# Layer one of a graph network: eight rows of every group are fetched by SyncE in place of GpSimd

## What is computed

```python
def _rgcn_layer(x, W, SW, b, src, dst, rel):
    xt = jnp.einsum('nd,rde->rne', x, W)          # 8 relations
    msg = xt[rel, src]                            # one row of 128 for each edge
    agg = jax.ops.segment_sum(msg, dst, num_segments=x.shape[0])
    return jax.nn.relu(agg + x @ SW + b)
x = _rgcn_layer(entity_emb, w1, sl1, b1, src, dst, edge_type)
x = _rgcn_layer(x, w2, sl2, b2, src, dst, edge_type)
```

## Time and profile before

| | us |
|---|---|
| median of 3 executions | 8923.19 |
| lowest, highest | 8923.06, 8924.19 |
| profiled execution, total | 8924.33 |
| profiled execution, span from first to last instruction | 8922.3 |
| of it layer one's gathers, first start to last start | 120.9 to 2196.9 |

### The profile page before, as it was taken

How to read it: one execution, slowest core, us unless ns; L and a number is a source line. 1 busy time by engine, 2 the same in 40 slices (tenths; PEclk the granted TensorE clock), 3 DMA queues, 4 the chain that set the end, 5 groups by cost and what they waited for, 6 DMA issues and landing times. The chain is left out here.

```text
span 8922.3 us, 172430 instructions
## 1 busy us (share of the span) xinstructions
PE 6527.5 (73%) x29604; PEld 5175.7 (58%) x29605; DVE 5892.7 (66%) x18026; ACT 2572.9 (29%) x6876; POOL 6456.8 (72%) x6759
## 2 busy tenths in 40 slices
PE   6555555555788888888888988888745677666667
PEld 4433333333555555555688888888734566666555
DVE  4444444444566666666688888888854776766767
ACT  3111111111011111111355555555433333333322
POOL 6777777776777777777677777777757777777752
PEclk7566666666555555555555555555556777877778
DMA  5222222222222222222455555555435666666652
GB/s 199 61 65 67 66 65 66 66 65 64 54 63 62 62 63 62 62 63 62 102 137 136 136 136 136 136 136 136 121 81 126 154 154 152 156 154 154 154 139 77
DMA packets 1031683, 926.16 MB, mean 104 GB/s; under 512 B 210913, under 2 KB 911477, under 8 KB 1031495
## 3 DMA queue, kind: packets, MB, share of 16 engines
q0 software_dynamic: 214496, 443.25, 18.3%
q1 hardware_dynamic: 627671, 341.67, 15.1%
q10 hardware_dynamic: 189400, 139.98, 7.8%
HBM read 734.34 MB, written 192.49 MB: 104 GB/s over the span
## 5 line engine op out<-in xcount | busy, mean ns | idle before, releaser
L599 PE MATMUL stage_ps_agg<-stage_hot,stage_msg 128*128 128x128 f32 x6656 | 1587.4, 414 | 1221.6 <-DMA stage_msg<-xt,stage_index 890.7
L599 PEld LDWEIGHTS stage_ps_agg<-stage_hot,stage_msg 128*128 128x128 f32 x6656 | 1377.5, 306 | 1519.2 <-issue 662.4
L1174 POOL DMA_INDIRECT big<-q,stage_index x1664 | 1597.2, 960 | 547.3 <-issue 489.0
L1631 POOL DMA_INDIRECT slots<-big,stage_index x1664 | 1603.2, 963 | 510.6 <-issue 442.0
L588 POOL DMA_INDIRECT stage_msg<-xt_next,stage_index x1664 | 1570.7, 944 | 531.0 <-issue 520.3
L588 POOL DMA_INDIRECT stage_msg<-xt,stage_index x1664 | 1570.3, 944 | 530.3 <-issue 487.6
L631 DVE TENSOR_TENSOR big<-big,stage_ps_agg 128x128 f32 x3328 | 951.7, 286 | 1350.5 <-PE stage_ps_agg L599 989.8
L577 ACT ACTIVATE stage_index<-big 128x4 int32 (+1 forms) x832 | 170.3, 205 | 3607.3 <-PE stage_ps_agg L599 3509.1
L1668 PE MATMUL stage_ps_val<-nodes_a,big 128*128 x3328 | 672.4, 366 | 656.8 <-ACT big L1594 635.1
L1668 PEld LDWEIGHTS stage_ps_val<-nodes_a,big 128*128 128x128 f32 x3328 | 592.4, 267 | 719.0 <-issue 718.3
L1684 PE MATMUL stage_ps_sums<-stage_hot,big 128*128 128x128 f32 x4160 | 754.9, 345 | 112.0 <-DVE big L1804 107.1
(11 more groups left out here) (306 smaller groups left out, 9675.2 us busy)
## 6 DMA issues: line engine op xcount, KB each, us to landing
big<-slots SPq DMA_DIRECT2D x1976, 66.0 KB
big<-in_edge_attr_dram SPq DMA_DIRECT2D x1664, 64.0 KB
stage_trow<-targets ACTq DMA_DIRECT2D x830, 128.0 KB
stage_msg<-xt,stage_index POOLq DMA_INDIRECT x1664
stage_msg<-xt_next,stage_index POOLq DMA_INDIRECT x1664
big<-q,stage_index POOLq DMA_INDIRECT x1664
slots<-big,stage_index POOLq DMA_INDIRECT x1664
xt_next<-stage_xo SPq DMA_DIRECT2D x98, 256.0 KB, 2.9
```

The costliest lines, as they stand in the source:

```text
L599: last = self.nc.tensor.matmul(self.ps[h][:, j, :], self.msg[q][:, j, :], self.hot[h][:, j, :], start=True, stop=True)
L1174: pool.indirect_dma_start(qrow[q][:, j * D:(j + 1) * D], None, d["q"], bass.IndirectOffsetOnAxis(ap=index[q][:, j:j + 1], axis=0))\
L1631: pool.indirect_dma_start(d["slots"], bass.IndirectOffsetOnAxis(ap=index[q][:, j:j + 1], axis=0), total[q][:, j, :], None).then_inc(s_sc[q ...
```

## The change

`prepare` makes a second small table: VectorE copies the last eight (`SIDE`) lanes' row numbers of every tile from `row` into `side` as integers, and SyncE writes that to HBM as its last transfer. `first_layer` begins with a SyncE transfer that brings the eight numbers of each group's fourth tile into one partition of on-chip memory (`side_rows`).

In layer one's `gather` the fourth indirect DMA of a group covers partitions 0 to 119. SyncE fetches the other eight rows (`load_side_rows`): it waits until the slot is free, twice loads four row numbers into registers, and issues eight DMAs of one row each on a semaphore of the slot. TensorE waits for that semaphore besides the gathers'. SyncE's program for the layer is now written by `walk_edges` as well, and the store of a job stands in it two groups after ScalarE's copy. Layer two is as before.

```diff
+SIDE = 8
 # prepare, SyncE
+        sp.wait_ge(s_v, SIDED)
+        sp.dma_start(d["side"].rearrange("(c p) l -> p c l", p=P), side[:, :, :]).then_inc(s_tab, 16)
...
-        sp.wait_ge(s_tab, 32)
+        sp.wait_ge(s_tab, 48)
 # prepare, VectorE
         v.wait_ge(s_v, NUMBERED)
+        nc.vector.tensor_copy(side[:, :, :], row[:, :, P - SIDE:P]).then_inc(s_v, 1)
 # Layer.gather
                 for j in range(G):
-                    pool.indirect_dma_start(self.msg[q][:, j, :], None, self.xt,
-                                            bass.IndirectOffsetOnAxis(ap=self.index[q][:, j:j + 1], axis=0))\
+                    rows = P - self.side if j == G - 1 else P
+                    pool.indirect_dma_start(self.msg[q][0:rows, j, :], None, self.xt,
+                                            bass.IndirectOffsetOnAxis(ap=self.index[q][0:rows, j:j + 1], axis=0))\
                         .then_inc(self.s_msg[q], 16)
+    def load_side_rows(self, sp, x):
+
+        q = x.slot()
+        sp.wait_ge(self.s_freed, x.at() + 1)
+        for k in range(0, SIDE, G):
+            r = offsets(self.nc, mybir.EngineType.SP, self.t["side_rows"], x.at() * SIDE + k, G, W * P * R - 1)
+            for j in range(G):
+                p = P - SIDE + k + j
+                sp.dma_start(self.msg[q][p:p + 1, G - 1, :], self.xt[bass.ds(r[j], 1), :]).then_inc(self.s_side[q], 16)
 # Layer.sum_messages
         pe.wait_ge(self.s_msg[q], x.turn() * (16 * G) + (16 * G + self.at[q]))
+        if self.side:
+            pe.wait_ge(self.s_side[q], x.turn() * (16 * SIDE) + 16 * SIDE)
 # first_layer, SyncE
+        sp.dma_start(t["side_rows"].rearrange("a (g l) -> a g l", l=SIDE),
+                     d["side"].rearrange("(g j) l -> j g l", j=G)[G - 1:G, :, :]).then_inc(s_rows, 16)
...
         sp.wait_ge(s_pad, 32)
-        sp.addr_align(256, max_nops=1)
-        with sp.Fori(0, JOBS) as s:
-            o = a.half_block(mybir.EngineType.SP, s)
-            sp.wait_ge(s_out, s * 2 + 2)
-            sp.dma_start(d["xt_next"][bass.ds(o, HALF), :], xo[:, :]).then_inc(s_st, 16)
+
+        def group(x):
+            if x.edge():
+                a.load_side_rows(sp, x)
+            if x.job(STORE):
+                s = x.job_at(STORE)
+                o = a.half_block(mybir.EngineType.SP, s)
+                sp.wait_ge(s_out, s * 2 + 2)
+                sp.dma_start(d["xt_next"][bass.ds(o, HALF), :], xo[:, :]).then_inc(s_st, 16)
+
+        walk_edges(sp, group, LAYER_MARKS, JOB_REACH, SLOTS)
```

More of the change, by code:

```diff
@@ L121, in prepare @@
     wrel = m.sb("wrel", [D, R * D])
+    side = m.sb("side", [P, KC, SIDE], I32)
     xin = [m.sb(f"xin{q}", [P, 2, D]) for q in range(XS)]
@@ L139, in prepare @@
     CH = [(c0, min(G, KC - c0)) for c0 in range(0, KC, G)]
-    BEGUN, ROW, WN, SIZED, SMALLER, WVAL, RANKED, TVAL, START, MARKED, NUMBERED = range(1, 12)
+    BEGUN, ROW, WN, SIZED, SMALLER, WVAL, RANKED, TVAL, START, MARKED, NUMBERED, SIDED = range(1, 13)
     ROW_COUNT, SIZES, FIRSTS, TILES, TURNED, ENDS = 2, 3, 4, 5, 6, 7
@@ L555, with __init__ @@
 class Layer:
-    def __init__(self, nc, m, t, d, xt):
+    def __init__(self, nc, m, t, d, xt, side=0):
         self.nc, self.t, self.d = nc, t, d
@@ L570, in __init__ @@
         self.s_msg = t["landed"]
+        self.side = side
+        if side:
+            self.s_side = [m.sem(f"a_side_rows{q}") for q in range(SLOTS)]
         self.at = add_landed(t, [TURNS * G * 16] * SLOTS)
@@ L644, in first_layer @@
 def first_layer(nc, m, t, d, x_in, w_all, self_w, bias):
-    a = Layer(nc, m, t, d, d["xt"])
+    a = Layer(nc, m, t, d, d["xt"], SIDE)
     ones16 = m.sb("ones16", [P, 1], BF16)
@@ L658, in first_layer @@
     RELU, OUT = (p + SLOTS for p in (2, 4))
+    STORE = OUT + 2
+    s_rows = m.sem("a_side_table")
     COLS = R * D // 2
@@ L2100, in build @@
         t["row"] = t["big"][:, 13 * K:14 * K].bitcast(I32)
+        t["side_rows"] = t["big"][0:1, 5 * K:5 * K + GROUPS * SIDE].bitcast(I32)
         t["link_m"], t["link_s"] = (t["big"][0:G * H, 13 * K + a * K // 2:13 * K + (a + 1) * K // 2]
@@ L2105, in build @@
             "tiles": nc.dram_tensor("tiles", (2, K), I32).ap(),
+            "side": nc.dram_tensor("side", (K, SIDE), I32).ap(),
             "xt": nc.dram_tensor("xt", (W * P, R * D), FP32).ap(),
```

## The result

| | before | changed |
|---|---|---|
| median of 8 executions each, us | 8924.39 | 8950.98 |
| lowest, highest | 8921.02, 8927.41 | 8948.53, 8954.3 |
| profiled execution, total | 8924.33 | 8951.83 |
| its span | 8922.3 | 8949.7 |

The ratio is 1.0031, with a 95% interval from 1.0022 to 1.0039: slower by 26.6 us, which is more than the 0.2% (17.8 us) that can be told from none. The forecast was 8929.3, no difference that counts, with a range from 8903 to 9015; the time lies in the range, 21.7 us over the forecast.

What follows compares the result with a forecast made beforehand. GpSimd's gather queue was taken to bound layer one. 8924.33 + 0 (gather) + 1.5 (preparation) + 4.3 (start) + 0.3 (clears) = 8930.4 us on the profiled execution, so 8929.3 at the median; range 8903 to 9015, the forecast's own 8923 to 8945.

Steps and rivals of the forecast that it cites:

- The bound: Layer one: GpSimd's gather queue never stands still, 4.99 us for a group of four tiles, 416 groups.
- The shorter gather's saving: Layer one's fourth gather on GpSimd, 120 rows in place of 128: saving taken as zero.
- The two ends: Fourth gather's cost over 416 groups: from 24.5 us saved, by the row, to 85 us added, by the first indirect transfer.
- rival 1: Layer one's gathers: GpSimd's cost goes by the row, -24.5 us, total 8904.8 us; chance 0.16.
- the nearer 49-row transfer's +18: Preparation's 49-row indirect transfer, 962 ns: +18 ns for a gather, 7.5 us over 416 groups.
- the first one's +204: Kernel's first indirect transfer, 49 rows, 1148 ns: +204 ns for a gather, 85 us over 416 groups.
- rival 3: Layer one's fourth gather: an odd row count costs GpSimd 50 to 204 ns more, +21 to +85 us; chance 0.08.
- SyncE's turn: SyncE's work per group in layer one: 4.61 us, under GpSimd's 4.99 by 0.38, so it hides.
- rival 2: Layer one, SyncE's loop: SyncE becomes the bound when a group passes 4.99 us, +29 to +133 us; chance 0.25.
- TensorE's new wait: Layer one: single rows land 6.3 us after the buffer is free, needed at 18; nothing paid in steady state.
- The start: Layer one's first groups: SyncE begins after x's copy, so GpSimd stops once at group 4, +4.3 us (3 to 7).
- The preparation and the clears: Row-number write behind SyncE's last table store, +1.5 us; five more semaphores cleared, +0.3 us.

Runs made afterwards that it cites:

- The side part: Against the changed kernel, all four gathers have 128 rows again and SyncE's eight rows go to an unread tile; 8927.96 us, 1.0007 to the kernel before.
- the early start: Against the changed kernel, SyncE's loop waits only for the row-number table, the wait for x's copy moved behind it; 8944.83 us, 1.0028 to the kernel before.

## Why the prediction was right, and where it missed

- **The bound** was right: GpSimd's queue, in the changed kernel as before, 0.30 us between gathers and 4.6 us of waits in 1800 us. So the length of a gather counts in full, 416 times a group's difference.
- **The shorter gather's saving, taken as zero, was the mis-sized term.** It costs 49 ns a group, 20.6 us, and this is 20.6 of the 21.7 us between forecast and result. The two ends stood in the text: against rival 1's saving by the row it was right (64 rows in place of 128 save 40 ns), and the value lies between the nearer 49-row transfer's +18 and the first one's +204. The choice of zero came from the packets. They were read rightly, as the unchanged 214496 show, and the Trainium skill's rule of the largest divisor (page DMA: Bandwidth & Descriptors, section Why a DMA increments its semaphore by 16 and not by 1) says the same of the shares, and the packet sizes for 126, 120, 104 and 124 rows agree with it. But neither says what such a count costs GpSimd: an equal number of packets isn't an equal time to write them. The row that was nearest in kind, a count that 16 doesn't divide, said +18 and not 0; with it the forecast would have been 8936.8, and still 14 us short. So this term was rival 3, at its lower edge of 50 ns and 8950, to which I had given 0.08.
- **SyncE's turn, 4.61 us,** was 4.88, and the 0.38 us of room were 0.16 beside a group of 5.04, or 0.10 beside one of 4.99. It was sized too small by its loads: 3.26 for 3.39 of transfers, 1.14 for 0.83 of loads, 0.33 for 0.24 of a store, 0.14 for 0.15. A transfer took 213 ns at the median where I had 240, and a load 467 at the median (543 in the first stretch) where I had 295. The 4.615 us of the first stretch look like the forecast, but hold no store, and the forecast without its store is 4.37. The load's median of 647 wasn't reached. The Trainium skill (page DMA: Bandwidth & Descriptors, section Latency and other measured facts) gives a floor of about 600 ns for a load of registers; it isn't one here, with 301 at the least. That SyncE would hide was right, at 97% of its time and not 92%; rival 2 was nearer than forecast.
- **TensorE's new wait** is unpaid in the steady state, as said: from 300 to 2100 us it waits for no single row. Before that it does, 73.1 us in 20 waits from 120 to 300 us, while SyncE makes up for its late start, and GpSimd stops only at group 4.
- **The start,** forecast as 4.3 us (3 to 7), cost 4.64 us in the profiled execution and 3.2 to 3.8 in four others, and index and restart came 2.1 and 2.8 us later than forecast, mostly because all of it was shifted by the preparation.
- **The preparation and the clears,** forecast as 1.5 + 0.3, cost 2.2 us in the profiled execution and 0.6 to 1.6 in four others, all against the one profiled execution before.
- **The chances.** 0.35 for slower by over 0.2% rested mostly on rival 2, and the result came by rival 3. The range held it; the forecast's own range, 8923 to 8945, did not, and "no difference that counts" did not come. The range held it because rivals 2 and 3 had stretched it to 9015, and the one of them that came had the smallest chance of all, 0.08. That the time lies inside is luck in good part.

## What to carry to other kernels

An indirect gather issued by GpSimd is paid by the piece: 128 rows cost 944 ns and 64 rows 913, so taking rows away from a full gather saves next to nothing, and only fewer gathers would. If a gather must be shorter, its rows should be a multiple of 16. Before work is moved from the engine that is the bound to one that sleeps, measure what the bound's remaining instruction costs in its new shape: here the helper hid, though more narrowly than planned, and the instruction that was helped became longer.

## What the runs showed of the hardware

- A row count that 16 doesn't divide makes an indirect gather longer: 120 rows 982 to 993 ns, 104 rows 982, 126 rows 996, beside 938 for 112 and 944 to 953 for 128. 124 rows take 1295. Packet sizes show equal shares, as many as the largest number up to 16 that divides the rows, filled up to sixteen with four-byte pieces, and beyond 128 rows and pieces each costs some 0.9 ns.
- SyncE issues a one-row transfer with a computed address in 213 ns, and with register work and gaps 0.41 us on average; a load of four row numbers takes 301 ns at the least and 467 at the median, 543 in the stretch in which it never waits.
- In single executions every gather takes 3 ns more (947 for 944), in both layers, and the whole execution is 15 to 19 us longer: the side part's profiled one (8942.93, median 8927.96) and the early start's (8963.58, median 8944.83). A term of 20 us should not be read from one execution alone.
- Twice the whole program took 11.56 ms instead of 8.92, the kernel before included, with gathers of the same length and sequencers that halt for up to 1.4 us. There the side part costs 6% (1.0594), since SyncE becomes the bound, where it otherwise costs 6.8 us (1.0007). What makes the setting is open.
